# Two halves of a group as one step: a new order of the work on TensorE, ScalarE and VectorE in a graph message kernel

## The reference

```python
row, col = src, dst
msg_in = concat([x[row], x[col], edge_attr], axis=-1)    # 100000 x 384
h = msg_in @ W + b
h = (h - mean(h)) * rsqrt(var(h) + 1e-5) * gamma + beta    # per edge, over 128
msg = relu(h)
out = segment_sum(msg, row, num_segments=6250)
return layernorm(x + out)
```

## Time and profile before

| | |
|---|---|
| median of 3 runs | 1759.11 us (1758.96 to 1759.6) |
| profiled execution | 1758.61 us, its span 1756.8 us |
| PE busy | 1201.1 us, 68% |
| PE weight load busy | 1049.7 us, 60% |
| DVE busy | 949.3 us, 54% |
| ACT busy | 711.4 us, 40% |
| POOL busy | 771.9 us, 44% |
| mean granted TensorE clock | 0.812 of full |
| DMA | 215 MB, 123 GB/s over the span |

### The profile page before, as it was taken

The page is one execution under the profiler, slowest core; times in us unless marked ns, Lnnn a source line. Parts: engine busy times, 40 slices in busy tenths (PEclk is TensorE's granted clock), DMA queues, the critical chain, the costliest instruction groups (busy, mean ns, idle before and its releaser), DMA issues.

```text
span 1756.8 us, 36181 instructions
## 1 busy us (share of the span) xinstructions
PE 1201.1 (68%) x9913; PEld 1049.7 (60%) x9914; DVE 949.3 (54%) x2787; ACT 711.4 (40%) x2814; POOL 771.9 (44%) x810
## 2 busy tenths in 40 slices
PE   6598776666766666766666666667666667656775
PEld 5455666655666556666566666566555656655662
DVE  7623355545555445554455555455455455538997
ACT  3223343433434333443334333344344344335766
POOL 0335544455444455444554444554445554450003
PEclk9767777878878788787888778788888777878998
DMA  7665455344443444444444443444444444312322
GB/s 213 170 129 137 127 154 147 111 127 131 129 115 116 124 131 129 120 115 125 126 130 130 115 128 113 131 130 127 112 120 126 131 128 128 111 54 80 92 65 73
DMA packets 192458, 215.22 MB, mean 123 GB/s; under 512 B 51350, under 2 KB 141802, under 8 KB 192272
## 3 DMA queue, kind: packets, MB, share of 16 engines
q1 hardware_dynamic: 166236, 160.39, 35.1%
q0 software_dynamic: 25088, 51.83, 8.5%
q10 hardware_dynamic: 948, 0.79, 0.2%
HBM read 144.85 MB, written 68.06 MB: 121 GB/s over the span
## 4 chain that ended last, share of the span: by engine, by line
PE 39%; another core or an unknown queue 24%; issue 18%; ACT 10%; DVE 6%; DMA 2%; DVEq 1%; SPq 0%; ACTq 0%
PE bank L962 11%; PE bank L940 7%; PE bank L916 7%; ACT late L1183 5%; PE bank L856 5%; PE bank L930 3%; PE bank L969 2%; ACT turn L1145 1%; DVE late L1580 1%; PE bank L846 1%; DMA tabB<-room 1%; PE bank L844 1%; ACT late L1189 1%; DVEq L493 1%
## 5 line engine op out<-in xcount | busy, mean ns | idle before, releaser
L683 POOL DMA_INDIRECT rows<-p,pos_idx x784 | 756.0, 964 | 825.3 <-ACT p L1149 535.0
L1145 ACT COPY turn<-bank 128x512 f32<-128x512 f32 x196 | 115.0, 587 | 688.0 <-remote 523.3
L962 PE MATMUL bank<-wc,turn 128*128 128x128 f32 x1552 | 297.2, 351 | 66.9 <-ACT turn L1145 59.9
L940 PE MATMUL bank<-room 128*128 x2592 | 246.4, 250 | 106.6 <-issue 61.4
L962 PEld LDWEIGHTS bank<-wc,turn 128*128 128x128 f32 x1552 | 257.4, 251 | 88.1 <-ACT turn L1145 79.3
L940 PEld LDWEIGHTS bank<-room 128*128 128x128 bf16 x2592 | 204.3, 115 | 128.0 <-issue 117.6
L1183 ACT ACTIVATE late<-room 128x128 f32<-128x128 f32 x864 | 256.4, 303 | 2.7 <-issue 1.3
L916 PE MATMUL bank<-late 128*128 128x129 f32 x1472 | 230.3, 299 | 33.9 <-issue 31.4
L1580 DVE SCALAR_TENSOR_TENSOR late<-room,late,floor 128x128 f32<-128x128 f32 x864 | 248.1, 349 | 0.4 <-issue 0.3
L916 PEld LDWEIGHTS bank<-late 128*128 128x128 f32 x1472 | 207.5, 214 | 26.4 <-issue 26.0
L1175 ACT COPY room<-bank 128x512 bf16<-128x512 bf16 x216 | 127.0, 588 | 223.9 <-remote 128.8
(11 more groups left out here) (240 smaller groups left out, 1256.1 us busy)
## 6 DMA issues: line engine op xcount, KB each, us to landing
p<-in_edge_attr_dram SPq DMA_DIRECT2D x98, 512.0 KB
room<-rows SPq DMA_DIRECT2D x256, 129.0 KB
near_bc<-near SPq DMA_DIRECT2D x98, 256.0 KB
late<-rows SPq DMA_DIRECT2D x176, 129.0 KB
rows<-p,pos_idx POOLq DMA_INDIRECT x784
win<-tabB SPq DMA_DIRECT2D x196, 31.5 KB
rows<-fill SPq DMA_DIRECT2D x24, 193.5 KB
tabB<-room SPq DMA_DIRECT2D x12, 384.0 KB, 3.8
```

What stands on the lines that cost most here:

```text
L683: nc.gpsimd.indirect_dma_start(rows_ap, bass.IndirectOffsetOnAxis(pos_idx[:, k, j:j + 1], 0), stage[:, k, j, :], None).then_inc(st_free[k] ...
L940: mm = pe.matmul(bank[A_BANK + b2][:, jj * D:(jj + 1) * D], selT[b2][:, jj * P:(jj + 1) * P], tabA[:, bass.ds(at[jj // UJ], 1), part, :], ...
L962: pe.matmul(bank[H_BANK + h][:, t * D:(t + 1) * D], eT[h][:, t * P:(t + 1) * P], wc[:, 2, :], start=(t == 0), stop=False, skip_group_check ...
L1145: nc.scalar.copy(eT[h], bank[E_BANK][:]).then_inc(eT_ready, 1)
```

## The change

From group 13 on (`BY_GROUP`, the third group in which pairs run) each of TensorE, ScalarE and VectorE has a `pairs_step` in place of the two half steps: the same instructions for both halves and both pairs of a group, in another order. GpSimd's scatter is cut in two from the same group on: it issues four DMAs when the first half is staged and TensorE has multiplied both halves, and four more when the second half is staged.

```diff
+        BY_GROUP = LEAD // 2 + 2
...
+            def scatter(g, k, halves=False):
                 pool.wait_ge(pos_ready, g + 1)
                 pool.wait_ge(lo_ready, g + 1)
-                early = isinstance(g, int) and g == 0
-                pool.wait_ge(st_ready, 2 * g + (1 if early else 2))
+                if halves and g > 0:
+                    pool.wait_ge(h_done, 2 * g + 2)
+                pool.wait_ge(st_ready, 2 * g + (1 if halves else 2))
                 settle()
                 for j in range(COLS):
-                    if early and j == COLS // 2:
-                        pool.wait_ge(st_ready, 2)
+                    if halves and j == COLS // 2:
+                        pool.wait_ge(st_ready, 2 * g + 2)
+                        settle()
...
+                def pairs_step(g, k, u):
+                    s = 2 * g - LEAD
...
+                    pe.wait_ge(n_sel, s + 3)
+                    if g + 1 < NG:
+                        ranks_from_base(g + 1, slot(k, 1))
+                    turn_selectors(s, s % HS_RING, True)
+                    turn_edges(g, k, u, 1)
+                    turn_selectors(s + 1, (s + 1) % HS_RING, True)
+                    edges_times_w(g, k, 0)
+                    edges_times_w(g, k, 1)
...
+                        turn_edges(g + 1, slot(k, 1), u + (k + 1) // RING, 0)
+                    select_a(s, s % HS_RING, at_a)
+                    select_a(s + 1, (s + 1) % HS_RING, at_b)
+                    for i in range(1 if g == NG - 1 else 2):
+                        for jj in range(SJ):
+                            sum_tile(s + 1 + i, (s + 1 + i) % HS_RING, jj, True)
...
+                def pairs_step(g, k, u):
+                    s = 2 * g - LEAD
+                    if g > BY_GROUP:
+                        stage_rows(g - 1, slot(k, -1), 0)
+                    copy_edges(g, 0)
+                    copy_selT(s, s % HS_RING)
+                    copy_edges(g, 1)
+                    if g > BY_GROUP:
+                        squares(s - 1, (s - 1) % HS_RING)
+                        roots(s - 1, (s - 1) % HS_RING)
+                    copy_selT(s + 1, (s + 1) % HS_RING)
+                    stage_rows(g - 1, slot(k, -1), 1)
+                    squares(s, s % HS_RING)
+                    roots(s, s % HS_RING)
+                    number_rows(g, k, u)
...
+                def pairs_step(g, k, u):
+                    s = 2 * g - LEAD
...
+                    selectors(*pair_at(s), iota_ps, True)
...
+                    if g > BY_GROUP:
+                        add_pair(*pair_at(s - 1))
+                    add_pair(*pair_at(s))
+                    for v in range(2):
+                        add_run(s, s % HS_RING, at_a, v)
+                    for v in range(2):
+                        add_run(s + 1, (s + 1) % HS_RING, at_b, v)
+                    if g + 1 < NG:
+                        dst_selectors(g + 1, k1, u1)
+                    root_inverse(s, s % HS_RING)
+                    messages(s, s % HS_RING)
+                    dve.wait_ge(n_selTc, s + 3)
+                    if g + 1 < NG:
+                        rank_products(g + 1, k1, ranks_ps)
+                    if g + 2 < NG:
+                        block_onehot(g + 2, slot(k, 2), iota_ps[:, 0:BK])
+                    selectors(*pair_at(s + 1), iota_ps, True)
+                    if g + 1 < NG:
+                        rank_sums(g + 1)
+                    root_inverse(s + 1, (s + 1) % HS_RING)
+                    if g + 1 < NG:
+                        positions(g + 1, k1, u1)
+                    messages(s + 1, (s + 1) % HS_RING)
```

More of the change, by code:

```diff
@@ L425, in pair_of, with pair_at @@
             return s, s % HS_RING, s // HS_RING * 2, s // HS_RING
+        def pair_at(s):
+            return s, s % HS_RING, s // HS_RING * 2, s // HS_RING
+        BY_GROUP = LEAD // 2 + 2
         def pair_trips(eng, step):
@@ L672, in settle @@
                 pool.sem_inc(s_turn, 1)
-            def scatter(g, k):
+            def scatter(g, k, halves=False):
                 pool.wait_ge(pos_ready, g + 1)
                 pool.wait_ge(lo_ready, g + 1)
-                early = isinstance(g, int) and g == 0
-                pool.wait_ge(st_ready, 2 * g + (1 if early else 2))
+                if halves and g > 0:
+                    pool.wait_ge(h_done, 2 * g + 2)
+                pool.wait_ge(st_ready, 2 * g + (1 if halves else 2))
                 settle()
                 for j in range(COLS):
-                    if early and j == COLS // 2:
-                        pool.wait_ge(st_ready, 2)
+                    if halves and j == COLS // 2:
+                        pool.wait_ge(st_ready, 2 * g + 2)
+                        settle()
                     nc.gpsimd.indirect_dma_start(rows_ap, bass.IndirectOffsetOnAxis(pos_idx[:, k, j:j + 1], 0),
@@ L687, in _ @@
             with pool.If_eq(groups_without_window(pool), 0):
-                every_group(lambda g, k, u: scatter(g, k))
+                every_group(lambda g, k, u: scatter(g, k, g == 0 or g >= BY_GROUP))
             with pool.Else():
@@ L973, in _ @@
                 ranks(0, 0)
+                regs_b = [pe.alloc_register(f"pe_blk_b{v}") for v in range(2)]
+                def pairs_step(g, k, u):
+                    s = 2 * g - LEAD
+                    if g == BY_GROUP:
+                        turn_edges(g, k, u, 0)
+                        for jj in range(SJ):
+                            sum_tile(s, s % HS_RING, jj, True)
+                    pe.wait_ge(n_sel, s + 3)
[6 more added lines that the diff above has]
+                    edges_times_w(g, k, 1)
+                    at_a = entry(pe, regs, blk_i, s + 1, NB - 1)
+                    at_b = entry(pe, regs_b, blk_i, s + 2, NB - 1)
+                    if g + 1 < NG:
[3 more added lines that the diff above has]
+                    for i in range(1 if g == NG - 1 else 2):
+                        for jj in range(SJ):
+                            sum_tile(s + 1 + i, (s + 1 + i) % HS_RING, jj, True)
                 def step(g, k, u):
+                    if g >= BY_GROUP:
+                        pairs_step(g, k, u)
+                        return
                     for h in range(2):
@@ L1216, in _ @@
                 every_group(step)
+                stage_rows(NG - 1, (NG - 1) % RING, 0)
                 stage_rows(NG - 1, (NG - 1) % RING, 1)
+                squares(FUSED - 1, (FUSED - 1) % HS_RING)
+                roots(FUSED - 1, (FUSED - 1) % HS_RING)
             with act.Else():
@@ L1604, in _ @@
                 dst_selectors(0, 0, 0)
+                regs_b = [dve.alloc_register(f"dve_blk_b{v}") for v in range(2)]
+                def pairs_step(g, k, u):
+                    s = 2 * g - LEAD
+                    k1, u1 = slot(k, 1), u + (k + 1) // RING
+                    selectors(*pair_at(s), iota_ps, True)
+                    at_a = entry(dve, regs, blk_i, s - 3, NB - 1)
+                    at_b = entry(dve, regs_b, blk_i, s - 2, NB - 1)
+                    if g > BY_GROUP:
[18 more added lines that the diff above has]
+                    root_inverse(s + 1, (s + 1) % HS_RING)
+                    if g + 1 < NG:
+                        positions(g + 1, k1, u1)
+                    messages(s + 1, (s + 1) % HS_RING)
                 def step(g, k, u):
+                    if g >= BY_GROUP:
+                        pairs_step(g, k, u)
+                        return
                     last = isinstance(g, int) and g == NG - 1
@@ L1670, in _ @@
                 every_group(step)
+                add_pair(*pair_at(FUSED - 1))
             with dve.Else():
```

## The result

The changed kernel takes 2049.62 us (median of 5 runs, 2048.83 to 2057.11) where the kernel before took 1758.96 beside it (5 runs, 1756.9 to 1759.6): a ratio of 1.1674, 95% interval 1.165 to 1.170, slower. The profiled execution took 2057.11 us with a span of 2055.3, 298.5 us more than the span before.

What follows compares the result with a forecast made beforehand. Bound: a ring of waits, 15.58 us per period, with TensorE's signals held during each scatter. New period 11.75 + 1.9 + 4.44 = 18.09; 84 x 2.51 = +211 on 1758.61 gives 1970 us, range 1810 to 2060 (eight in ten: from 1690).

Steps and rivals of the forecast that it cites:

- the ring of waits: Loop period: scatter's first DMA to release 11.72, then ScalarE's copies, squares and staging to the next DMA 3.92; 15.64 us.
- The hold: While a scatter's indirect DMAs are in flight, TensorE's signals don't reach other engines; 11.75 us from first DMA to release.
- the release: Moment at which the engines that wait for TensorE go on after a scatter, 1.8 us after its last DMA is done.
- The 3 us after which I took signals for held: Start of the held stretch, some 3 us after a scatter's first DMA; what TensorE finishes earlier still gets through.
- The rival without a hold: Scatter is no cause, only the half steps' crossings; TensorE becomes the bound, -343 us, 1416 us; chance 0.08.
- One run of eight per group, second half and first half: GpSimd's second four DMAs of g - 1, then first four of g, in one run: still one held stretch, 11.75 us.
- Two holds per group: Rival: edge multiplication's signal is held, so the next group's first four DMAs wait; period 21.1, +464, 2220 us; chance 0.07.
- the signals get through: Rival: TensorE's results come out during the hold, ScalarE copies and squares in it; period 14.05, 1630 us; chance 0.17.
- The wait for selectors: VectorE's selectors wait for a message sum signalled only at the release; selectors, ranks and turned selectors add 1.9 us.
- Release to DMA: From the release to the next scatter's first DMA: 1.9 for the selector chain plus 4.44 for ScalarE's, where 3.92 stood.
- TensorE's part: Ranks and turned selectors on TensorE behind the release: 0.75 us at the high clock, twice that at the low, taken as 1.1.
- The second copy: Second of ScalarE's two copies after the release, taken as back to back, 0.48 us apart, 0.96 together.

## Why the prediction was right, and where it was off

The direction and the range were right, and so was the ring of waits behind them; the size came out 88 us short.

**The hold** is there on chips B, C and D: 11.75 us from the first DMA to the release in the changed kernel too, and with two DMAs more 14.4. "What TensorE signals doesn't reach the others" was half of it: TensorE's own work crawls as well. Whether its instructions start late, run slowly or signal late can't be told apart here. The 3 us after which I took signals for held are not a fixed edge: on D a signal got through 4.24 us after the first DMA. The rival without a hold (1416 us) is false on B, C and D. On A nothing is held, but there the new order with the scatter whole was 3.6% slower and not faster; the changed kernel itself wasn't timed there.

The rule of the Trainium skill (SBUF — State Buffer, Who interferes with whom) that a DMA never contends with a compute engine stands in a section on the ports to SBUF. Chip A agrees with it. On C two more DMAs stall VectorE and ScalarE 2.7 us longer, so there engines and DMAs do not run free of each other; through what they are coupled no run shows, so the ports need not be it.

**One run of eight per group, second half and first half**, held: 1003.28 to 1012.13, then 8.86 us idle. Two holds per group did not come, nor did the signals get through.

**The wait for selectors** held: VectorE's selectors are the first work after the release, TensorE and ScalarE follow. Taking that wait away gave back 144 us on B.

**The sizes.** Release to DMA was forecast as 6.34 and is 6.92. TensorE's part was mis-sized: 1017.20 - 1015.78 = 1.42 for 1.1, since the clock in that stretch is 0.50 and I had taken a value near the mean. The second copy starts 0.85 after the first, not 0.48, as it waits for edges that TensorE turns in the same stretch. The other differences (signals and selectors, squares, root, second copy, staging and its 0.81 to the DMA) come to -0.1 together. Over 78 periods 0.6 us is 46 us of the 88 that the forecast lacks.

**What the sum had left out.** The last five groups have a period of 23 us. In that stretch the selectors take turns in four buffers and no longer in five, so that a step's second selectors wait for a sum of the same step, after the hold:

```profile
1809.04 0.69 DVE L1646 TENSOR_TENSOR late<-bank,room 128x512 f32<-128x512 f32 x1 [11.07 <-remote]
1813.71 0.69 DVE L1646 TENSOR_TENSOR late<-bank,room 128x512 f32<-128x512 f32 x1 [2.25 <-PE bank L923]
...
1815.92 0.59 ACT L1210 COPY room<-bank 128x512 bf16<-128x512 bf16 x1 [15.25 <-PE bank L937]
```

The line in the code was there to be read, and the same groups cost 26 us on A. Against 18.09 per period these five are 25 us more than forecast, and the change of order at the start (24.37 us for one period) makes most of the rest. One label was wrong: the DMA at 256.23 is the first of group 12's scatter and that at 1564.56 of group 96's; the 84 periods between them are right.

**The split.** I said that its DMAs would form runs of eight and leave the time as it is. In the new order that is so (whole scatter: same ratio). In the old order it saves 3.2% on D. So the one part of the change that is worth something there was the split, and together with the new order nothing of it is left.

## What to carry to other kernels

Where two engines are released at one moment, period after period at the same distance from a third one's DMAs, that moment is the clock of the loop: count what stands between it and the next DMA, and what TensorE must have finished before. Moving a DMA run earlier moves TensorE's unfinished work behind the release, so that what is saved ahead can come back whole (1.47 saved, 1.63 given back here). A rotation of buffers that makes an early instruction wait for the last one of the step before joins two chains into one, and the stretch in which the rotation shrinks has to be counted by itself. And before a wait is put down to a late signal, the rows of the engine that should have sent it are worth reading: here they showed that engine nearly standing. Last, a gain or a loss can belong to the chip: the same edit cost 3.6% on A and 16.5% on C.

## What the runs showed of the hardware

- The same kernel takes 1243.68 us on one chip and 1739 to 1759 on the others. The windows of the new order with the whole scatter, 400 to 1000 us, on A:

```profile
400.00:1000.00 600.00, 483.21 (x5208) 435.99 (x5207) 462.73 (x1330) 355.27 (x1450) 446.55 (x464) 0.99 0.65 186
```

  and on C:

```profile
400.00:1000.00 600.00, 339.69 (x2880) 305.15 (x2880) 258.41 (x736) 199.13 (x800) 251.56 (x258) 0.75 0.37 104
```

  In the same 600 us A does 1330 / 736 = 1.8 times as many instructions on VectorE, at nearly the full clock. What in the chip or its state makes the difference stays open.
- On B, from some 5 us after the first of a run of eight indirect DMAs, TensorE starts an instruction or a few per 1.4 us with no wait to be seen; the kernel before shows the same on the chip of the first comparison (825.34, 826.77, 829.67). There it is at full rate again 829.67 - 828.07 = 1.6 us after the last DMA is issued and done. VectorE and ScalarE go on 1.0 to 2.0 us after it, in runs of eight and ten; on D a release also came 0.31 us before the last DMA had started.
- An indirect DMA of 128 rows takes GpSimd about 0.96 us with 0.30 between two, on every chip; two more per group cost 2.49 us per period where GpSimd is the bound (A) and 2.8 where the hold is (C).
